# Two-layer graph attention, 4096 nodes: row maxima moved into the layer-0 attention; keys in parts and a 16-bit output projection in layer 1

## The reference

```
layer 0:  h = relu(layernorm(x)); data = h @ W.T + b, viewed (N, H, D)
          src, trg = data . src_proj, data . trg_proj            (N, H)
          e = leaky(src_i + trg_j, slope 0.01) + adj_ij;  scores = softmax_j(e)
          x = x + scores @ data                                  per head
layer 1:  h = relu(layernorm(x)); a = max(adj, I)
          q, k, v = h @ Wq, h @ Wk, h @ Wv                       per head
          att = softmax_j(q.k / 8 - 1e16 * (1 - a_ij))
          x = x + concat_heads(att @ v) @ Wo
```

## Time and profile before

| | |
|---|---|
| median of 3 runs (5012.5 to 5022.32) | 5021.12 us |
| the profiled execution, its own time | 5012.62 us |
| its span, first to last instruction | 5010.9 us |
| mean granted TensorE clock | 0.965 |
| PE busy | 4584.9 us, 91% |
| DVE busy | 3379.6 us, 67% |
| ACT busy | 3110.1 us, 62% |
| POOL busy | 3452.4 us, 69% |
| DMA | 583.29 MB, mean 116 GB/s |

### The profile page before, as it was taken

How to read it: one execution, slowest core, us unless ns; L and a number is a source line. 1 busy time by engine, 2 the same in 40 slices (tenths; PEclk the granted TensorE clock), 3 DMA queues, 4 the chain that set the end, 5 groups by cost and what they waited for, 6 DMA issues and landing times.

```text
span 5010.9 us, 128860 instructions
## 1 busy us (share of the span) xinstructions
PE 4584.9 (91%) x43282; PEld 2220.7 (44%) x43793; DVE 3379.6 (67%) x6969; ACT 3110.1 (62%) x5768; POOL 3452.4 (69%) x2969
## 2 busy tenths in 40 slices
PE   5679999999999878699999899999999999999998
PEld 2322222222222234245555555555555555555555
DVE  6868888888888633556656556557557557466565
ACT  3345555555555333167777677677687687677675
POOL 1157776676777500078878788788788788788786
PEclk8789999999999989789999999999999999999999
DMA  7743233233232234453523425325244334334334
GB/s 310 311 115 97 87 109 93 91 111 93 92 108 70 92 100 118 149 131 91 150 74 110 131 73 139 99 77 156 78 109 134 86 101 135 93 98 130 92 100 120
DMA packets 354936, 583.29 MB, mean 116 GB/s; under 512 B 31200, under 2 KB 219648, under 8 KB 337088
## 3 DMA queue, kind: packets, MB, share of 16 engines
q1 hardware_dynamic: 348992, 557.63, 37.4%
q0 software_dynamic: 5120, 16.78, 1.1%
q10 hardware_dynamic: 128, 0.13, 0.0%
HBM read 497.61 MB, written 76.82 MB: 115 GB/s over the span
## 4 chain that ended last, share of the span: by engine, by line
PE 37%; issue 4%; DMA 3%; SPq 3%; DVE 2%; ACT 1%; POOL 1%; DVEq 0%; ACTq 0%; POOLq 0%
PE d_gd L1475 9%; PE d_sc L1490 6%; PE d_sc L1491 6%; PE d_sc L1492 5%; PE d_acc L1509 3%; PE d_acc L1511 3%; PE d_acc L1519 3%; DMA d_KA<-scratch_kl 3%; PE d_misc L1534 2%; POOL d_PL L1264 1%; SPq L1152 1%; DVE d_junk L1359 1%; ACT d_PH L1305 1%; ACT d_PF L1301 1%; SPq L1153 1%
## 5 line engine op out<-in xcount | busy, mean ns | idle before, releaser
L1264 POOL TENSOR_TENSOR d_PL<-d_PF,d_PH 128x512 f16<-128x512 f32 x2048 | 2357.0, 1176 | 630.6 <-ACT d_PH L1305 628.3
L1359 DVE CUSTOM_DVE_ANT_0 d_junk<-d_gd,d_MR 128x512 bf16<-128x512 f32 x2112 | 1445.0, 690 | 779.2 <-PE d_gd L1475 712.2
L1301 ACT ACTIVATE d_PF<-d_sc 128x512 f32<-128x512 f32 x2048 | 1234.0, 603 | 767.4 <-remote 385.1
L709 DVE SCALAR_TENSOR_TENSOR b_P<-b_R,u,b_A 128x512 f32<-128x512 f32 x1792 | 1202.4, 743 | 217.8 <-ACT b_A L621 154.8
L1305 ACT ACTIVATE d_PH<-d_sc 128x512 f16<-128x512 f32 x2048 | 1239.6, 605 | 0.0
L750 PE MATMUL b_acc<-b_P,V 128*64 128x512 f32 x4096 | 943.2, 601 | 38.1 <-DVE b_P L709 25.3
L1475 PE MATMUL d_gd<-d_KA,d_QA 128*128 128x512 f16 x2112 | 817.7, 387 | 135.6 <-DVE d_gm L1359 47.5
L1490 PE MATMUL d_sc<-d_QA,d_KA 128*128 128x512 f16 x2048 | 783.6, 383 | 64.9 <-ACT d_PH L1305 37.3
L1491 PE MATMUL d_sc<-d_QL,d_KB 128*128 128x512 f16 x2048 | 781.8, 382 | 0.0
L1511 PE MATMUL d_acc<-d_V,d_PH 128*128 128x64 f16 x8192 | 643.4, 194 | 0.0
L1509 PE MATMUL d_acc<-d_V,d_PH 128*128 128x65 f16 x8192 | 642.4, 193 | 0.1
(11 more groups left out here) (128 smaller groups left out, 3916.5 us busy)
## 6 DMA issues: line engine op xcount, KB each, us to landing
d_stage<-in_adj SPq DMA_DIRECT2D x144, 512.0 KB, 4.3
d_V<-scratch_v SPq DMA_DIRECT2D x131, 520.0 KB, 4.3
a_rows<-in_adj SPq DMA_DIRECT2D x32, 2048.0 KB, 9.5
b_stage<-in_adjT SPq DMA_DIRECT2D x128, 512.0 KB, 3.6
d_MT<-scratch_mt SPq DMA_DIRECT2D x36, 1024.0 KB, 6.3
d_KA<-scratch_kh SPq DMA_DIRECT2D x66, 512.0 KB, 8.1
d_KA<-scratch_kl SPq DMA_DIRECT2D x66, 512.0 KB, 10.2
d_KB<-scratch_kh SPq DMA_DIRECT2D x264, 128.0 KB, 3.0
```

What stands on the lines that cost most here:

```text
L709: nc.vector.scalar_tensor_tensor(out=PT[:, m % P_STEPS, h, :], in0=R[:, par, h, :], scalar=T["u"][:, m, h:h + 1], in1=A[m % A_RING][:, :], ...
L1264: eng.tensor_tensor(PL[:, t % H_RING, :], PF[:, t % F_RING, :], PH[:, t % H_RING, :], ALU.subtract).then_inc(s_lowp if by_pool(t) else s_l ...
L1301: nc.scalar.activation(PF[:, t % F_RING, :], sc[t % 2][:, :], ACT.Exp, scale=EXP_SCALE)
L1359: nc.vector.tensor_tensor_reduce(out=junk[:, gi % 2, :], in0=gd[gi % 2][:, :], in1=MR[:, s, c * QB:(c + 1) * QB], scale=1.0, scalar=-3.0e3 ...
```

## The change

It has three parts and a few small ones.

1. `layer0_project` scans only the four row tiles of block 0 (all four loaded at the start) and stores 512 maxima itself, four bytes at a time. The other 28 tiles of the rows are scanned in `layer0_attention`: while query block nb is worked on, the rows of nb + 1 are loaded in 16 chunks of 128x1024 and reduced by VectorE, a chunk after the P tiles of steps 3, 4, 6, 7, ..., 24, 25. At load 15 SyncE waits for the maxima, stores them, waits for that, and loads `am`. The ring `D2` shrinks from 4 to 2, and x is stored and loaded at load 13 in place of 9.
2. In `layer1_attention` the keys `KA` are loaded in four parts, for the head pair after the next, as the parts come free (at steps 7, 15, 23, 31, ahead of `KB`). The guards begin at step 2 in place of 5. The queries' load stays at step 0. The last part of the mask of a query block is loaded at its own step 10. The mask's chunks are 128x512, 32 of them, in a ring of 6. The two heads' `crow` become one set of four matmuls of two columns.
3. The output projection takes 16-bit high and low halves: 12 matmuls in place of 4 float32 ones; `copy_turned` makes the two halves in two VectorE instructions, and the weights are split once at the stage's start, before the first guard.

```diff
-    STORE_LOAD = 9 ; D_RING = 4
+    STORE_LOAD = 13 ; D_RING = 2
+    CW = N // 4 ; CHUNKS = SUB * N // CW ; ROW_RING = 2
+    RANK_STEPS = [3 + 3 * ci // 2 for ci in range(CHUNKS)]
+    ROW_LOADS = [4 + 3 * ci // 4 for ci in range(CHUNKS)]
+    AMAX_LOAD = 15
...
+            def store_amax(nb):
+                wait_apart(sp, s_amax, nb + 1, s_passed)
+                sp.dma_start(DR["amax"][bass.ds(nb * QB + QB, QB)].rearrange("(t p) -> p t", p=P),
+                             T["amax"][:, bass.ds(nb * SUB + SUB, SUB)],
+                             allow_slow_non_contiguous=True).then_inc(s_amout, 16)
+                wait_apart(sp, s_amout, nb * 16 + 16, s_passed)
...
+            def rank_chunk(nb, ci):
+                s, c = divmod(ci, N // CW)
+                dve.wait_ge(s_row[ci % ROW_RING], ...)
+                nc.vector.reduce_max(part[:, s, c:c + 1], rows[:, ci % ROW_RING, :], AX.X).then_inc(s_rank, 1)
+                if ci == CHUNKS - 1:
+                    dve.wait_ge(s_rank, nb * CHUNKS + CHUNKS)
+                    nc.vector.reduce_max(T["amax"][:, bass.ds(nb * SUB + SUB, SUB)], part[:, :, :], AX.X).then_inc(s_amax, 1)
...
-    CW = 1024 ; FIRST_G = 5 ; S_RING = 3
+    CW = 512 ; FIRST_G = 2 ; S_RING = 6 ; MT_LATE = 10 ; O_SCALE = 16.0
-    CHUNK_STEPS = [FIRST_C + 5 * ci // 2 for ci in range(CHUNKS)]
+    CHUNK_STEPS = [FIRST_C + 5 * ci // 4 for ci in range(CHUNKS)]
...
-        def load_ka(sp, par, hp):
+        def load_ka(sp, par, hp, i):
+            cols = slice(i * PER * P, (i + 1) * PER * P)
             for x in range(2):
-                sp.dma_start(KA[0:D, par, x, :], DR["kh"][row:row + D, :]).then_inc(s_KA[par][x], 16)
-                sp.dma_start(KA[D:P, par, x, :], DR["kl"][row:row + D, :]).then_inc(s_KA[par][x], 16)
+                sp.dma_start(KA[0:D, par, x, cols], DR["kh"][row:row + D, cols]).then_inc(s_KA[par][i], 16)
+                sp.dma_start(KA[D:P, par, x, cols], DR["kl"][row:row + D, cols]).then_inc(s_KA[par][i], 16)
...
                             load_q(sp, par, nxt, nb if hp < HP - 1 else (nb + 1) % NB)
-                            load_ka(sp, par, nxt)
                         if mb % PER == PER - 1:
                             sp.wait_ge(s_S, nb * TILES + (hp * PAIR + 2 * (mb + 1) + CREDIT))
+                            load_ka(sp, hp % 2, (hp + 2) % HP, mb // PER)
                             load_kb(sp, nxt, mb // PER)
-                            if hp == HP - 1:
+                            if hp == HP - 1 and mb < NT - 1:
                                 load_mt(sp, (nb + 1) % NB, mb // PER)
+                        if step == MT_LATE and not first:
+                            load_mt(sp, nb, GROUPS - 1)
...
                 s, x, c = gi // (2 * MC), gi // MC % 2, gi % MC
-                if s == 0 and c == 0:
-                    if x == 0:
-                        pe.wait_ge(s_Q[par], count * 96 + 96)
-                    pe.wait_ge(s_KA[par][x], count * 32 + 32)
+                if gi == 0:
+                    pe.wait_ge(s_Q[par], count * 96 + 96)
+                if s == 0 and x == 0 and c % (MC // GROUPS) == 0:
+                    pe.wait_ge(s_KA[par][c // (MC // GROUPS)], count * 64 + 64)
...
-                    mm = nc.tensor.matmul(misc1[:, :], oN[:, c, s * P:(s + 1) * P], wo[:, c, :], ...)
+                    for a, b in TERMS:
+                        mm = nc.tensor.matmul(misc1[:, :], oN[:, a, c, s * P:(s + 1) * P], woS[:, b, c, :], ...)
```

More of the change, by code:

```diff
@@ L135, in _ @@
             sp.dma_start(bias[:, :], DR["b"].partition_broadcast(P)).then_inc(s_w, 16)
[L136 to L143, removed]
+            for s in range(SUB):
+                sp.dma_start(rows[s][:, :], DR["adj"][s * P:(s + 1) * P, :]).then_inc(s_row, 16)
+            sp.wait_ge(s_rank, SUB)
+            sp.dma_start(DR["amax"][0:QB].rearrange("(t p) -> p t", p=P), T["amax"][:, 0:SUB],
+                         allow_slow_non_contiguous=True).then_inc(s_amout, 16)
             sp.wait_ge(s_amout, 16)
@@ L152, in in_blocks @@
         def in_blocks(eng, body):
-            with eng.Fori(0, NB - 1) as g:
-                body(g, False)
+            body(0, False)
+            with eng.Fori(0, NB - 2) as i:
+                body(i + 1, False)
             body(NB - 1, True)
@@ L212, in rank @@
             def rank(g, s):
-                dve.wait_ge(s_row[s], g * 16 + 16)
-                nc.vector.reduce_max(T["amax"][:, bass.ds(g * SUB + s, 1)], rows[s][:, :], AX.X).then_inc(s_rank, 1)
+                if isinstance(g, int) and g == 0:
+                    dve.wait_ge(s_row, 16 * SUB)
+                    nc.vector.reduce_max(T["amax"][:, s:s + 1], rows[s][:, :], AX.X).then_inc(s_rank, 1)
             def store_v(g, s):
@@ L416, in layer0_attention @@
         MD = sb("b_MD", [P, SUB, P], BF16)
+        rows = sb("b_rows", [P, ROW_RING, CW])
+        part = sb("b_part", [P, SUB, N // CW])
         acc = [pb(f"b_acc{i}", [P, QB]) for i in range(HP)]
@@ L452, in layer0_attention @@
         s_md = sem("diagonal_masks_stored")
+        s_row = [sem(f"row_in{i}") for i in range(ROW_RING)]
+        s_rank = sem("chunk_ranked")
+        s_amax = sem("rows_ranked")
+        s_amout = sem("amax_stored")
         s_out = sem("x1_stored")
@@ L528, in body @@
                         load_r(nb + 1, 1 - par)
+                    for ci in range(CHUNKS):
+                        if not last and k == ROW_LOADS[ci]:
+                            if not (first and ci < ROW_RING):
+                                wait_apart(sp, s_rank, nb * CHUNKS + (ci - ROW_RING + 1), s_passed)
+                            load_rows(nb + 1, ci)
+                    if k == AMAX_LOAD and not last:
+                        store_amax(nb)
+                        if not first:
+                            wait_apart(sp, s_sub, nb * NT, s_passed)
+                        load_am(nb + 1, 1 - par)
                     if k == STORE_LOAD:
@@ L711, in body @@
                                                        op0=ALU.max, op1=ALU.mult).then_inc(s_P, 1)
+                    for ci in range(CHUNKS):
+                        if not last and m == RANK_STEPS[ci]:
+                            rank_chunk(nb, ci)
                     if m == DIAG_MAX:
@@ L1097, in layer1_attention @@
         cm = sb("d_cm", [P, 2, SUB])
[L1098 removed]
+        cmh = sb("d_cmh", [P, SUB, 2], F16)
         shift = sb("d_shift", [P, 1])
+        only = sb("d_only", [P, 2])
         idh = sb("d_idh", [P, P], F16)
@@ L1110, in layer1_attention @@
         s_set = sem("constants_set")
-        s_KA = [[sem(f"ka_in{i}{x}") for x in range(2)] for i in range(2)]
+        s_oNh = sem("normalised_high")
+        s_KA = [[sem(f"ka_in{par}{i}") for i in range(GROUPS)] for par in range(2)]
         s_Q = [sem(f"q_in{i}") for i in range(2)]
@@ L1191, in _ @@
                 load_chunk(sp, 0, ci)
-            load_ka(sp, 0, 0)
             load_q(sp, 0, 0, 0)
+            for i in range(GROUPS):
+                load_ka(sp, 0, 0, i)
             for ci in range(S_RING, CHUNKS):
@@ L1197, in _ @@
                 load_chunk(sp, 0, ci)
+            for i in range(GROUPS):
+                load_ka(sp, 1, 1, i)
             for i in range(GROUPS):
@@ L1252, in _ @@
             for par in range(2):
-                for x in range(2):
-                    sp.wait_ge(s_KA[par][x], 32 * (2 * NB + 1 - par))
+                for i in range(GROUPS):
+                    sp.wait_ge(s_KA[par][i], 64 * (2 * NB + 1))
                 sp.wait_ge(s_Q[par], 96 * (2 * NB + 1 - par))
@@ L1445, in body @@
                             mask_setup(nb + 1, (nb + 1) % NB)
-                        if step in CHUNK_STEPS:
-                            mask_chunk(nb + 1, (nb + 1) % NB, CHUNK_STEPS.index(step))
+                        for ci in range(CHUNKS):
+                            if step == CHUNK_STEPS[ci]:
+                                mask_chunk(nb + 1, (nb + 1) % NB, ci)
             body(0, True)
@@ L1548, in _ @@
                 guard(0, 0, gi, 0)
-            for x in range(2):
-                crow(0, x)
+            crow(0)
             def body(nb, first):
@@ L1575, in body @@
                         if mb == CROW_STEP:
-                            for x in range(2):
-                                crow(it, x)
+                            crow(it)
                         if step >= LAG:
```

93 lines of the change are left out of this document (54 added, 39 removed).

## The result

| | before | after |
|---|---|---|
| median of 8 runs (lowest to highest) | 5019.48 us (5012.5 to 5022.32) | 5033.6 us (5031.08 to 5040.35) |
| the profiled execution's span | 5010.9 us | 5032.8 us |
| mean granted TensorE clock | 0.965 | 0.963 |

The ratio is 1.0032, with a 95% interval of 1.0021 to 1.0043: 0.3% slower, just more than a measurement of this kernel can tell. The forecast was 5038, slower likelier than faster by a little.

The account below looks back on a forecast made before the run. TensorE was taken to bound layer-0 attention and the layer-1 loop, VectorE's scans to delay the first stage. Terms from -65 (projection) to +124 (query waits) summed to +17 on 5021: 5038 us, range 4955 to 5090.

Parts of the forecast that it names:

- (a): Layer-0 projection: with VectorE's scans of seven blocks gone, the first stage ends at 209.4 instead of 275.12, -65 us.
- the -47 bound: Layer-0 projection: smaller gain, -47 us, if TensorE's clock stays low in each block, some 3 us each.
- (b): Layer-0 attention: the added row-maximum chunks cost 1.4 us per block in seven blocks, +10, bounds 0 and +40.
- rival D: Layer-0 attention: VectorE becomes the bound, 5.5 us per block, up to 5086 us; chance 0.18.
- (c): Layer-1 loop: the first guard waits 3.75 us for queries; an ordinary change of head pair costs +5.15, 24 of them +124.
- key loads add 2.55: Layer-1 jumps: four key loads delay the last query load by 2.55 us, giving a wait of 5.75.
- B: Layer-1 guards: the wait for queries comes but the clock doesn't fall, or for under a microsecond; 4990 us, chance 0.25.
- rival C: Layer-1 guards: queries land before step 2 and cause no wait; 4838 us, chance 0.09.
- (d): Layer-1 loop: guards in 27 steps instead of 24 leave three fewer slow steps in 32 head pairs, -21 us.
- (e): Output projection: twelve 16-bit matmuls take 2.59 us where four took 3.51; -26 in the loop, -4 at the end.
- (g): Layer-1 mask chunks: halved ones are better bridged by the guard's two banks, 1.5 us each, -24, bounds -40 and 0.
- step (f): Layer 1: four `crow` matmuls fewer, 0.06 us each, half under ScalarE's step, -5.

Follow-up runs that it names:

- experiment 1: The changed kernel with the query loads issued a head pair early, at step 31 ahead of the key loads: 4863.0 us, ratio 0.9698.
- experiments 1 and 2: Beside experiment 1, its second is the changed kernel with query loads left in place and guards in steps 5 to 28, not 2 to 28: 4884.7 us.
- experiment 7: Kernel of experiment 1 with layer-0 row-maximum chunks at steps 5 to 25: 4852.9 us; then also guards from step 3, not 2: 4843.1 us.
- experiment 5: The kernel before with 155 semaphore increments nobody waits for added to SyncE's program in the last block of layer-0 attention: 4983.0 us, ratio 0.9933.

## Why the prediction was right or wrong

**(a) Projection: right.** -63.4 for -65. The turn of block 1 did not quite stay (57.09 for 54.90), the next came 28.5 later as forecast, and block 7 is turned at 188.52 (186). From block 1 on these transposes run at the higher level (1.09 for eight; block 0 has 1.94), so the -47 bound was never near:

```profile
32.74 1.94 PE L337 MATMUL a_tp<-identf,a_h 128*128 128x128 f32 x8 [9.23 <-ACT a_h L276]
...
57.09 1.09 PE L337 MATMUL a_tp<-identf,a_h 128*128 128x128 f32 x8 [3.12 <-ACT a_h L276]
...
188.52 1.09 PE L337 MATMUL a_tp<-identf,a_h 128*128 128x128 f32 x8 [1.56 <-ACT a_h L276]
```

**(b) Layer-0 attention: right in size, wrong in one cover.** +12.9 for +10. A chunk took 1.21 us (1.1), a block became 1.2 longer (1.4), 8.2 in seven, and the first one 4.8. But that SyncE's waits for the chunks sit four steps ahead, "which covers them", fails for the first chunk of each block. Its load stands in the queue behind the eight of `R`: in the second block it is issued at 426.66 and lands at 437.02, just behind the last of those (435.69), where the median load of rows takes 4.1, and VectorE waits 2.69 for it. Moving the chunks gave 8.4 back. The rival D, VectorE as the bound, did not come: blocks of 179.6 on average.

**(c) The guards' first wait: right, and it decided.** Three of its terms were off and nearly made up for each other. The ordinary wait was 4.5 on average (108.3 in 24) for 3.75: from `KB` to the last query load SyncE took 5.70 (3003.72 to 3009.42), where the earlier trace rows had 4.58, as two of its issues took 2.17 in place of 1.11. Behind the jumps it was 2.8 to 3.4 for 5.75: the step "key loads add 2.55" held SyncE's gap at the jump fixed, and it fell from 6.0 to 6.8 to 3.4 to 4.2. The prediction's sum has 1.9 for the clock in the 5.15 of a change (and in B's 24 x 1.9), a term that no run shows; the runs showed 1.7 for each of the 32 waits, 55.4 us in all (experiment 1), and "each followed by matmuls of 0.6" is nearly so: a stretch at the lower level follows 31 of the 32 waits, and none the wait of 3.76 at 2460.7. Thirty-two waits of 140.0 in sum against "31, over 110". In the first run, with almost all of that gone, the kernel lands at 4863, where the prediction had 4838 for its rival C.

**(d) Guards in 27 steps: right.** 21.6 for 21 (experiments 1 and 2), though experiment 7 suggests that the first of the three steps is worth little.

**(e) Output projection: over-sized.** 17 in all for 30, in a kernel without the waits. The matmuls fell as predicted, 3.7 a head pair; the error is that a head pair's gain was taken for the kernel's.

**(g) Mask chunks: wrong.** -24 was forecast and 0 found. The reading of the earlier trace rows, that 2.9 us more in head pair 2 is VectorE's longer instruction, took what happened beside the chunks for their effect: 1.2 of it stays with either size, and the rest went with other parts of the change, which were not told apart. Why a whole chunk takes 1260 ns in the loop and 749 at the stage's start no run shows. A whole chunk and its two halves take 1260 and 2 x 833 ns by their medians.

The balance of the edit without its wait, by what was measured: layer 0 -50.5, guards -21.6, output -17, chunks 0, SyncE's jump in the kernel before -35, the keys' waits that experiment 5 left -19.5. Sum -144 against 155 found (5018.1 to 4863.0). The 11 left hold the four `crow` matmuls fewer of step (f), which were not tried alone (20.4 to 12.9 us busy in all), and what the intervals hide: the 35 alone would be 28 by the spans, and 17 and 155 come from different chips.

So +17 was near the +14 in part by luck: (e) and (g) together gave 37 too much gain, and what was missing on the other side was that the kernel before loses some 30 us to SyncE's gaps at the jumps, which no longer hold up the keys once these are loaded early. Had the loop of the kernel before lain 155 instructions on (4983.0), the same change would have been 1% slower.

## What to carry to other kernels

When a load is made early, look at what else the same instruction waits for: here the guard's keys came a head pair ahead, its queries stayed behind four new issues in SyncE's queue, and one moved call was worth 171 us. Test a size in the kernel where it is to stand, as a gain measured elsewhere may be another mechanism's. And before 0.5% is put down to an edit, look at the engines' gaps at the loop's jumps in both traces: instructions added ahead of the loop moved them in two kernels here, SyncE's by 5 to 6 us a jump and TensorE's by some 3, and in the changed kernel they did not.

## What the runs showed of the hardware that was not expected

- At a jump of the layer-1 loop SyncE issued nothing for 6.0 to 6.8 us in the kernel before, and for 0.73 to 0.76 with the same loop 155 increments on (experiment 5), which changed the kernel by 35 us. The instruction queue's packets differ too (324 and 295).
- TensorE's stop at its jump went from 3.6 to 4.4 us up to 6.6 to 7.4 with 110 increments placed in an earlier stage. The loop became 16 us longer by it, and the increments themselves took 17.
- A 2 KB store of single floats took 10.6 us to land:

```profile
scratch_amax<-amax SPq DMA_DIRECT2D x8, 2.0 KB, 10.6
```

where the 16 KB row of the kernel before took 1.4. The trace of the kernel after has 528 packets of four bytes while the first of these stores is under way, and the room that the prediction gave it, some 20 us, was enough.
- Waits of 2.8 to 8.9 us cost another 1.7 us each, on average, with the lower clock behind 31 of 32. In the first run a guard that had waited 0.94 ran at the higher level:

```profile
2949.13 0.39 PE L1540 MATMUL d_gd<-d_KA,d_QA 128*128 128x512 f16 x1 [0.94 <-DMA d_QL<-scratch_ql]
```
